# Sixteen-head causal attention: units on 50 contraction rows of alternating partition halves, maxima in half steps, two bfloat16 mask products, three score banks

## What is computed

```python
q = x @ Wq;  k, v = split(x @ Wkv)          # 16 heads of 16 numbers each
dots = einsum('bhid,bhjd->bhij', q * 16 ** -0.5, k)
dots = where(causal, dots, -50000.0)        # key j counts for query i only if j <= i
attn = softmax(dots) ;  out = (attn @ v) @ Wo
```

## Time and profile before

| | us |
|---|---|
| median of three executions | 3226.88 (3223.44 to 3228.7) |
| span of the profiled execution, first to last instruction | 3218.2 |
| TensorE busy in the span | 2924.2 (91%) |
| VectorE, ScalarE, GpSimd busy | 1882.8, 1578.7, 382.5 |
| attention of layer 0, 187.85 to 621.65 us | 433.8 |
| in it: start and projections, to 239.16 | 51.3 |
| in it: from the first maxima to the last normalisation, 620.6 | 381.4 |

### The profile page before, as it was taken

How to read it: one execution, slowest core, us unless ns; L and a number is a source line. 1 busy time by engine, 2 the same in 40 slices (tenths; PEclk the granted TensorE clock), 3 DMA queues, 4 the chain that set the end, 5 groups by cost and what they waited for, 6 DMA issues and landing times. The chain is left out here.

```text
span 3218.2 us, 50056 instructions
## 1 busy us (share of the span) xinstructions
PE 2924.2 (91%) x17179; PEld 2052.1 (64%) x17181; DVE 1882.8 (59%) x4554; ACT 1578.7 (49%) x3849; POOL 382.5 (12%) x729
## 2 busy tenths in 40 slices
PE   7978999899999998758799999998999999959996
PEld 5746666546777777344577777764667777836664
DVE  5456555346777766777577777345667777332223
ACT  4403555426666661644466666233566666213331
POOL 4560000001111100000000000000111111012222
PEclk8998999999999999879899999998999999979998
DMA  4452221245444321005432321006544443341112
GB/s 123 121 171 64 44 55 28 76 158 162 124 146 145 121 88 39 1 20 160 130 86 68 86 68 35 20 10 195 171 138 126 150 125 104 118 159 34 34 35 92
DMA packets 242482, 308.23 MB, mean 96 GB/s; under 512 B 27261, under 2 KB 185085, under 8 KB 242096
## 3 DMA queue, kind: packets, MB, share of 16 engines
q1 hardware_dynamic: 235082, 285.50, 29.1%
q0 software_dynamic: 7152, 19.54, 2.1%
HBM read 231.31 MB, written 73.21 MB: 95 GB/s over the span
## 5 line engine op out<-in xcount | busy, mean ns | idle before, releaser
L2407 ACT ACTIVATE cond_p<-cond_p,cond_negm 128x128 f32<-128x128 f32 (+7 forms) x768 | 593.2, 775 | 408.4 <-DVE cond_negm L2438 407.5
L2388 PE MATMUL ps_o<-cond_pt,cond_v 128*64 128x256 f32 (+1 forms) x3840 | 478.2, 370 | 5.1 <-DVE attn_out L2474 0.5
L2368 PE MATMUL ps_s<-cond_k_high,cond_q_high 128*128 128x512 f32 (+5 forms) x1152 | 439.4, 387 | 16.8 <-DVE cond_negm L2438 8.3
L2438 DVE CUSTOM_DVE_ANT_0 cond_p<-ps_s,cond_side,cond_null_scores 128x128 f32<-128x128 f32 (+7 forms) x512 | 403.7, 811 | 28.1 <-PE ps_s L2369 22.6
L2369 PE MATMUL ps_s<-cond_k_both,cond_q_both 128*128 128x512 f32 (+5 forms) x1152 | 394.1, 344 | 0.0
L2378 PE MATMUL ps_t<-ident,cond_p 128*128 128x128 f32 x2304 | 348.8, 281 | 6.8 <-ACT cond_pt L2412 4.8
L2388 PEld LDWEIGHTS ps_o<-cond_pt,cond_v 128*64 128x64 f32 x3840 | 237.4, 136 | 180.4 <-issue 89.8
L2378 PEld LDWEIGHTS ps_t<-ident,cond_p 128*128 128x128 f32 x2304 | 250.0, 140 | 106.0 <-issue 77.1
L1507 ACT ACTIVATE attn_pt<-ps_t 128x512 f32<-128x512 f32 (+3 forms) x384 | 173.0, 490 | 237.9 <-PE ps_t L1468 174.6
L2368 PEld LDWEIGHTS ps_s<-cond_k_high,cond_q_high 128*128 128x128 f32 x1152 | 219.9, 191 | 40.1 <-DVE cond_negm L2438 22.3
L2446 DVE COPY cond_pt<-ps_t 128x512 f32<-128x512 f32 (+1 forms) x240 | 140.4, 585 | 166.3 <-PE ps_t L2378 164.6
(11 more groups left out here) (503 smaller groups left out, 4682.1 us busy)
## 6 DMA issues: line engine op xcount, KB each, us to landing
mqa_q_halves<-cond_q_cut SPq DMA_DIRECT2D x96, 512.0 KB, 4.7
cond_q_both<-mqa_q_halves SPq DMA_DIRECT2D x384, 128.0 KB, 3.2
cond_q_high<-mqa_q_halves SPq DMA_DIRECT2D x192, 128.0 KB, 3.0
cond_side<-in_fside_16xSxS SPq DMA_DIRECT2D x32, 512.0 KB, 7.2
moe_experts<-in_L_ffn_W SPq DMA_DIRECT2D x16, 1024.0 KB, 12.2
cond_side<-in_fside_16xSxS SPq DMA_DIRECT2D x32, 448.0 KB, 5.6
cond_side<-in_fside_16xSxS SPq DMA_DIRECT2D x32, 384.0 KB, 5.0
cond_side<-in_fside_16xSxS SPq DMA_DIRECT2D x32, 320.0 KB, 4.6
```

Source lines behind the costliest of these rows:

```text
L2368: nc.tensor.matmul(out, c32(a.Q1[i][:, h, s * P:(s + 1) * P]), c32(a.K1[:, keys]), start=True, stop=False)
L2388: last = nc.tensor.matmul(sums[u % ON][h * HD:(h + 1) * HD, s0 * P:2 * P], a.V[:, b * QB + kb, :], PT[c % PT_SLOTS][:, (2 * h + s0) * P:(h ...
L2407: nc.scalar.activation(p, p, ACT.Exp, bias=negm[u % SMALL][:, r:r + 1], scale=-1.0, accum_out=rsum[u % SMALL][:, r:r + 1]).then_inc(exped, 1)
L2438: nc.vector.tensor_tensor_reduce(out=probs(u, r, 0, q + 1), in0=m.S[k % 2][:, row_offset(L):row_offset(L) + L], in1=toep_back(u, h, L) if ...
```

## The change

A unit takes the three combinations high-high, high-low and low-high, 48 partitions, and two rows for the maximum: 50 rows. Even units lie on partitions 0 to 49, odd ones on 64 to 113, of two buffers instead of three (so four units' places). Ones are written on partitions 32 to 63 and 96 to 127 of `KS` before the first load, and nothing is cleared. The maxima products run over 48 rows, the scores over 50. The mask becomes bfloat16 and is kept for each half as two products of 64 rows. A job `max` is cut in two, `open` and `max`: one head each for query blocks 0 to 3, the first 512 and the remaining keys for blocks 4 to 7; the pace allows one after h = 0 as well. Scores take turns on three banks, of which the third is one of the two sums' banks, and `attend` on the one that is left waits for the copy (`save`) of the group before. `PT` has four buffers. Unit u + 4 is loaded when unit u's scores are done, in nine transfers.

```diff
-                jobs.append(("max", u, qb, first))
+                jobs += [("open", u, qb, first), ("max", u, qb, first)]
                 if turn is not None and len(jobs) == turn:
                     jobs.append(("turn", u, 0))
             if qb == 3:
-                turn = len(jobs) + 3
+                turn = len(jobs) + 6
         return jobs + [("turn", u, 1)]
 
     def share(job):
-        return 0 if job[0] == "turn" else (job[2] + 1) * (2 if job[2] < 4 else 1)
+        if job[0] == "turn":
+            return 0
+        return job[2] + 1 if job[2] < 4 else 4 if job[0] == "open" else job[2] - 3
 
     first_unit = maxima(0)
-    upper = [job for job in first_unit if job[:3] == ("turn", 0, 1) or (job[0] == "max" and job[2] >= 4)]
+    upper = [job for job in first_unit if job[:3] == ("turn", 0, 1) or (job[0] != "turn" and job[2] >= 4)]
...
-                    while h and queue and taken < pace * given:
+                    while queue and taken < pace * given:
...
+    HALF, PARTS, PTS = 64, 3, 4
+    DATA = PARTS * HD
...
-    QS = [m.sb(f"attn0_q{i}", [P, 2, G4, GRP], F32, at + i * 16384) for i in range(3)]
-    KS = [m.sb(f"attn0_k{i}", [P, G4, S], F32, at + i * 16384) for i in range(3)]
-    PT = [m.sb(f"attn0_pt{i}", [P, G4, GRP], F32, at + i * 8192) for i in range(3)]
+    QS = [m.sb(f"attn0_q{i}", [P, 2, G4, GRP], F32, at + i * 16384) for i in range(2)]
+    KS = [m.sb(f"attn0_k{i}", [P, G4, S], F32, at + i * 16384) for i in range(2)]
+    PT = [m.sb(f"attn0_pt{i}", [P, G4, GRP], F32, at + i * 8192) for i in range(PTS)]
...
-    mask = m.sb("attn0_mask", [P, P], F32, at + 512)
-    unit = m.sb("attn0_unit", [P, P], F32, at + 1024)
+    causal = m.sb("attn0_causal", [HALF, 2, P], F32, at)
+    mask = m.sb("attn0_mask", [P, 2, P], BF16, at + 1024)
+    unit = m.sb("attn0_unit", [P, 2, P], BF16, at + 1536)
...
+    scores_in = [m.T[0], m.T[1], m.O[1]]
+    TN = len(scores_in)
+
+    def rows_of(u):
+
+        return u // 2 % 2, u % 2 * HALF
...
+                it, b = u // B, u % B
+                i, low_row = rows_of(u)
+                if u >= 4:
+                    sp.wait_ge(scored, score_of[("scores", u - 4, 1, QB - 1, G4 - 1)] + 1)
...
+                for p, (q_half, k_half) in enumerate(((0, 0), (0, 1), (1, 0))):
+                    part = slice(low_row + p, low_row + DATA, PARTS)
...
+            sp.wait_ge(cleared, 4)
             load(0)
...
-            nc.gpsimd.memset(causal[:, :], 0.0).then_inc(masked, 1)
+            nc.gpsimd.memset(causal[:, :, :], 0.0).then_inc(masked, 1)
             pool.wait_ge(masked, 1)
-            nc.gpsimd.affine_select(out=causal[:, :], in_=causal[:, :], compare_op=ALU.is_ge, fill=FAR,
-                                    base=0, pattern=[[-1, P]], channel_multiplier=1).then_inc(masked, 1)
+            for i in range(2):
+                nc.gpsimd.memset(KS[i][32:64, :, :], 1.0).then_inc(cleared, 1)
+                pool.wait_ge(cleared, 2 * i + 1)
+                nc.gpsimd.memset(KS[i][96:128, :, :], 1.0).then_inc(cleared, 1)
+                pool.wait_ge(cleared, 2 * i + 2)
+            nc.gpsimd.affine_select(out=causal[:, :, :], in_=causal[:, :, :], compare_op=ALU.is_ge, fill=FAR,
+                                    base=0, pattern=[[HALF, 2], [-1, P]], channel_multiplier=1).then_inc(masked, 1)
+            pool.wait_ge(masked, 2)
...
-            pool.wait_ge(padded, 3)
-            for i in range(3):
-                nc.gpsimd.memset(QS[i][64:P, :, :, :], 0.0).then_inc(cleared, 1)
-                nc.gpsimd.memset(KS[i][64:P, :, :], 0.0).then_inc(cleared, 1)
-            pool.wait_ge(cleared, 6)
-            for i in range(3):
-                nc.gpsimd.memset(KS[i][64:66, :, :], 1.0).then_inc(cleared, 1)
-            pool.wait_ge(cleared, 9)
...
-                if step[0] == "max":
+                if step[0] in ("open", "max"):
                     _, u, qb, first = step
-                    if qb == 0 and first == 0:
-                        pe.wait_ge(stacked[u % 3], 16 * (12 * (u // 3 + 1) + u // 3))
-                    out, L = slot(step), (qb + 1) * P
-                    for h in range(first, first + (2 if qb < 4 else 1)):
-                        queries = r(QS[u % 3][:, qb // 4, h, qb % 4 * P:(qb % 4 + 1) * P])
-                        at_ = (h - first) * GRP
-                        for lo in range(0, L, GRP):
-                            hi = min(lo + GRP, L)
-                            nc.tensor.matmul(out[:, at_ + lo:at_ + hi], queries, r(KS[u % 3][:, h, lo:hi]),
-                                             start=True, stop=(hi < L))
-                        last = nc.tensor.matmul(out[:, at_ + L - P:at_ + L], r(unit[:, :]), r(mask[:, :]), start=False, stop=True)
-                    last.then_inc(made, 1)
+                    i, low_row = rows_of(u)
+                    data, half = slice(low_row, low_row + DATA), slice(low_row, low_row + HALF)
+                    second, L = int(step[0] == "max"), (qb + 1) * P
+                    if step[0] == "open":
+                        if qb == 0 and first == 0:
+                            pe.wait_ge(stacked[u % 4], 16 * 9 * (u // 4 + 1))
+                        out = slot(("max", u, qb, first))
+                    else:
+                        out = m.S[slot_of[step] % 2]
+                    h = first + second if qb < 4 else first
+                    queries = r(QS[i][data, qb // 4, h, qb % 4 * P:(qb % 4 + 1) * P])
+                    lo, hi = (0, L) if qb < 4 else (second * GRP, L if second else GRP)
+                    at_ = second * GRP if qb < 4 else 0
+                    ends = hi == L
+                    last = nc.tensor.matmul(out[:, at_ + lo:at_ + hi], queries, r(KS[i][data, h, lo:hi]), start=True, stop=not ends)
+                    if ends:
+                        for j in range(2):
+                            last = nc.tensor.matmul(out[:, at_ + L - P:at_ + L], unit[half, j, :], mask[half, j, :],
+                                                    start=False, stop=(j == 1))
+                    if second:
+                        last.then_inc(made, 1)
...
-                    i, s0 = score_of[step], live(G, kb)
+                    k, s0 = score_of[step], live(G, kb)
+                    i, low_row = rows_of(u)
+                    rows, half = slice(low_row, low_row + DATA + 2), slice(low_row, low_row + HALF)
                     if kb == 0 and h == 0:
                         pe.wait_ge(max_rows[G], 32 * (u + 1))
-                    if i >= 2:
-                        pe.wait_ge(exped, i - 1)
-                    out = m.T[i % 2]
-                    last = nc.tensor.matmul(out[:, s0:GRP], r(KS[u % 3][:, h, kb * P:(kb + 1) * P]), r(QS[u % 3][:, G, h, s0:GRP]),
+                    if k >= TN:
+                        pe.wait_ge(exped, k - TN + 1)
+                    out = scores_in[k % TN]
+                    last = nc.tensor.matmul(out[:, s0:GRP], r(KS[i][rows, h, kb * P:(kb + 1) * P]), r(QS[i][rows, G, h, s0:GRP]),
                                             start=True, stop=(kb < 4 * G))
                     if kb >= 4 * G:
-                        last = nc.tensor.matmul(out[:, s0:s0 + P], r(mask[:, :]), r(unit[:, :]), start=False, stop=True)
+                        for j in range(2):
+                            last = nc.tensor.matmul(out[:, s0:s0 + P], mask[half, j, :], unit[half, j, :], start=False, stop=(j == 1))
...
-                    if kb == 0 and gi >= 2:
-                        pe.wait_ge(saved, gi - 1)
+                    if kb == 0 and gi >= 1:
+                        pe.wait_ge(saved, gi)
                     for h in range(G4):
                         col = (u // B * G4 + h) * VS
-                        last = nc.tensor.matmul(m.O[gi % 2][h * W:(h + 1) * W, s0:GRP], VA[:, u % B * QB + kb, col:col + W],
-                                                PT[i % 3][:, h, s0:GRP], start=(kb == 0), stop=(kb == 4 * G + 3))
+                        last = nc.tensor.matmul(m.O[0][h * W:(h + 1) * W, s0:GRP], VA[:, u % B * QB + kb, col:col + W],
+                                                PT[i % PTS][:, h, s0:GRP], start=(kb == 0), stop=(kb == 4 * G + 3))
...
-            nc.vector.tensor_copy(r(unit[:, :]), m.ident[:, :]).then_inc(constants, 1)
+            nc.vector.tensor_copy(unit[0:HALF, 0, :], m.ident[0:HALF, :]).then_inc(constants, 1)
+            nc.vector.tensor_copy(unit[HALF:P, 0, :], m.ident[0:HALF, :]).then_inc(constants, 1)
+            nc.vector.tensor_copy(unit[0:HALF, 1, :], m.ident[HALF:P, :]).then_inc(constants, 1)
+            nc.vector.tensor_copy(unit[HALF:P, 1, :], m.ident[HALF:P, :]).then_inc(constants, 1)
             dve.wait_ge(masked, 2)
-            nc.vector.tensor_copy(r(mask[:, :]), causal[:, :]).then_inc(constants, 1)
+            nc.vector.tensor_copy(mask[0:HALF, :, :], causal[:, :, :]).then_inc(constants, 1)
+            nc.vector.tensor_copy(mask[HALF:P, :, :], causal[:, :, :]).then_inc(constants, 1)
```

(24 more changed lines are left out.)

29 lines of the change are left out of this document (9 added, 20 removed).

## The result

The changed kernel takes a median of **3348.11 us** (four runs, 3333.17 to 3359.59), the kernel before 3227.79 beside it: ratio **1.0376** [1.0344, 1.0408]. The forecast was 3225 us, the range 3196 to 3250, with 0.38 on slower. The size lies far outside.

What follows compares the result with a forecast made beforehand. TensorE's order of work was taken as the bound. Steady units -3.6, unit 0 +1, ahead of it 0, unit 7 -3.8 and start +4.5 gave -1.9 us: median about 3225 us, range 3196 to 3250.

Steps and rivals of the forecast that it cites:

- slower: Whole kernel: a time more than 0.2% above the kernel before, chance 0.38.
- the rival of the clock: Steady units: each would run like unit 0 (63.0 against 44.1 us) at a lower clock, 3340 us; chance 0.02.
- Masks: Steady unit: each mask becomes two bfloat16 products and delays the next float32 weight load, +2.2 us, bounds 0 and +3.5.
- Side by side: Steady unit: plain products of opposite halves run together, half the gain lost to VectorE waits, -1.6 us, bounds 0 and -4.2.
- the faster rival: Scores and maxima: the other half's weights load early, masks cost nothing extra, pairs start under 0.02 us apart; 3204 us, chance 0.25.
- Third bank: Scores, with fourth `PT`: less waiting for ScalarE, -1.6 us a steady unit (bounds 0 and -3.8), -5.4 in unit 7.
- Half steps: Maxima jobs cut into `open` and `max`: said to fill the gap of TensorE's wait for ScalarE, with no cost of their own.
- two slots, no slack: Group 1's plain key blocks: VectorE's maxima need 3.1 us against TensorE's 3.3, so half the side-by-side gain becomes waits.
- Changes of shape: Steady unit: 6 to 8 switches between 64-row and 128-row products at 0.04 us each, +0.4 us, bounds 0 and +1.
- The start: Stage's start: GpSimd's mask comes behind four fills, so cutting and value copies begin later, +3.8 to +6.1 us, taken +4.5.
- the sum of the steady unit: Units 1 to 6: 2.2 - 1.6 - 1.6 + 0.4 = -0.6 us each, six of them -3.6 us.
- The 8.7 us around the span: Whole kernel: time added to the profiled execution's forecast 3216.3 us to give a median of about 3225 us.

Runs made afterwards that it cites:

- filled halves: Changed kernel with zeros and ones behind each half's 48 data rows, maxima over 62 rows, scores over 64, and the mask made before the fills: 3321.74 us.
- short reductions: Changed kernel with VectorE's maxima taken over the first 128 columns only and the exponential of 1e-6 times its input: 3231.79 us.
- the one with whole masks and whole jobs: Changed kernel with halves filled to 62 and 64 rows, one 128-row mask product per mask pair, and the order of the kernel before: 3479.66 us.
- the last run: Changed kernel with halves filled to 62 and 64 rows, maxima jobs whole in the order of the kernel before, mask pairs kept: 3243.74 us, ratio 1.0073.

## Why the prediction was wrong

**The failing step is the rival of the clock**, set at 0.02: "Waits in group 1 won't reach that." Its chance was too low. That its price (3340 us) came so near 3348 is luck: it put 19 us on each of six units and nothing elsewhere, where 13.0 to 16.3 us a unit, 23.3 in unit 0, 10.1 in unit 7 and 6.2 at the start were measured. The argument looked only at TensorE's idle time. It read clock 0.57 from a stretch with 8.0 us of work in 14.3 and asked whether the waits of a unit would become as long. They did not, and the clock fell all the same: the change also takes TensorE's products from 128 rows to 48 and 50, and the prediction costed that at nothing, since the other rows are zeros. The kernel before with 66 rows shows that narrower products alone can do it (3355 us); filled halves and short reductions show that in the changed kernel rows and waits for VectorE have a share each. The Trainium skill ("TensorE: Matmul & The Clock Gate", What's actually happening) has the clock set by how busy TensorE has been. Read as busy time, this case does not agree: 7.00 of 7.00 us busy and clock 0.50 in the changed kernel, 78.43 of 78.43 us and 0.54 in the one with whole masks and whole jobs.

**Masks.** Forecast +2.2 a unit, bounds 0 and 3.5. On whole rows a bf16 mask costs and saves nothing in a steady unit (43.3 against 43.2); the pair was not timed alone at full clock, but it is within the next sum.

**Side by side.** Forecast -1.6, with pairs 0.11 us apart. They start 0.00 to 0.01 apart in the changed kernel and in the last run, which the prediction had named as the sign of the faster rival. Masks, side by side and changes of shape together were +1.0; at full clock they are 40.4 - 43.2 = -2.8, with the fourth `PT` and the nine transfers in it, which no run takes apart. That rival's mechanism was right; it had 0.25, and the clock covered it. The rule of the Trainium skill ("TensorE: Matmul & The Clock Gate", Part 3) that products in different row groups start about 4 ns apart agrees with these rows.

**Third bank.** Forecast -1.6 a unit, measured -0.9; in unit 7 -5.4, measured -3.0. The wait of the loads for ScalarE doesn't go: it falls from 3.8 us to 1.8 (1.0 and 0.8, the bank named `ps_o` counted in), in unit 7 from 13.3 to 8.6, and only part of that was time.

**Half steps.** Priced at nothing and given credit for filling the gap; measured +1.9 a unit at clock 1.00, up to +3.4 at 0.96. The prediction had "two slots, no slack" in the term above, but did not ask how long each slot is held.

**Changes of shape.** Priced at 0.04 us, from the step into `attend`, which has 128 rows like its neighbour. From half to whole array it is about 0.3 at half clock (0.73 less 0.43). With 6 to 8 of them a unit the term stays small; with one at each mask it rules. The rule of the Trainium skill ("TensorEngine Tiling (Array Packing)", Key Properties) that changing the tiling mode drains TensorE agrees with the 0.73 us.

**The start.** Forecast +4.5 (3.8 to 6.1), came to +6.2, just outside. The first cut at 204.60 lies within 203.1 to 205.4; the first copy of values (217.26) just past 214.8 to 217.1. What was new there is VectorE's cast of 3.53 us beside GpSimd's fill, which hid behind the fills' 14 us. Behind the wait of 3.70 us, four projections take 2.48 us and the next four 3.12, at clock 0.75 and 0.69 (four take 1.88 us at 1.00).

**The whole.** The six units were to take 43.5 us each. By the last run's 40.4 and the half steps' 1.9, the changed kernel at clock 1.00 would take about 42.3, an estimate. So the sum of the steady unit was about right, partly by errors that cancel, and what a unit of 57.1 to 60.4 us has above 42.3, 14.8 to 18.1 us, is the clock's.

**The 8.7 us around the span.** They are not the start and end of the program. For every execution that has both figures, the time is 1.6 to 1.8 us above the span (3349.59 and 3347.9 for the changed kernel), so the execution with the span of 3218.2 took about 3220 us, an estimate, and was itself faster than the median. The forecast of 3225 doesn't hang on it, since it adds -1.9 us to the median.

What stays open: a kernel with whole rows in units 0 and 7, where the clock fails first, and halves between was not tried, nor a third slot of maxima for the halves. Narrower products alone cost the kernel before its clock; how rows, products side by side and waits are weighed against each other can't be told from these runs.

## What to carry to other kernels

Before you narrow a product, read the granted clock and ask what keeps it: rows of zeros may be what holds TensorE at 2.4 GHz. Packing two narrow products side by side gains at an equal clock (17.6 us of 82 at half clock, up to 2.8 of 43 at full clock), but no kernel here that packs and does the whole work beat the one before: the best, with rows filled and waits shortened, is 0.7% behind. Take a change like this apart: one of its four parts, the third bank, was worth 0.5% by itself, and the rest cost more than it.

## What was not expected of the hardware

- The same 286 or 287 products a unit, with the same sums and waits no longer than before, ran at clock 1.00 over 128 or 96 rows and at 0.53 to 0.86 over 66.
- Once fallen, the clock stayed at 0.50 through a stretch in which TensorE was busy without a gap (405 to 419 us), and through all of a unit of 58 us (unit 7 with 66 rows, and with short reductions).
- VectorE's cast of 64x128 numbers took 3.53 us beside a fill of GpSimd's that took 3.50, and 0.22 us without one (filled halves). The Trainium skill ("SBUF — State Buffer", SBUF: two separate sides) has it that of an instruction of GpSimd's and certain ones of VectorE's the one that starts first blocks the other to its end; the two rows agree.
- GpSimd's fill of 4096 numbers a partition takes 3.50 to 3.51 us over 2 or 64 partitions and over 32 (the changed kernel).
